# A state-space mixer and a mixture of experts: convolution taps read from PSUM, and the order of one mixer step changed on every engine

## The reference

```
h = layernorm(x) * (1 + ca) + sa
x = x + ga * mixer(h)            # state-space mixer
h = layernorm(x) * (1 + cb) + sb
x = x + gb * moe(h)              # 64 experts, top 8 of 4 of 8 groups, and a shared one

mixer(h): xn = rmsnorm(h); z, xBC, dt = xn @ in_proj.T      # 1024 | 1280 | 16 columns
  xBC = silu(sum_k pad(xBC)[k : k+L] * conv_w[:, k] + conv_b)   # 4 taps along the sequence
  xs, B, C = xBC (1024 | 128 | 128);  dt = softplus(dt + dt_bias)
  y = ssd(xs * dt, dt * A, B, C) over chunks of 128 tokens; y += D * xs
  y = rmsnorm(y * silu(z));  return h + y @ out_proj.T
moe(h): scores = sigmoid(h @ w_router); pick 8 experts; sum of weighted silu(gate) * up @ down
```

## Time and profile before

| what | value |
|---|---|
| median of three runs | 6409.36 us |
| the profiled execution | 6412.97 us |
| its span, first to last instruction | 6411.1 us |
| TensorE busy | 5781.9 us (90%) |
| VectorE busy | 3957.1 us (62%) |
| POOL busy | 3763.9 us (59%) |
| ScalarE busy | 2733.7 us (43%) |
| mean granted TensorE clock | 0.951 |

### The profile page before, as it was taken

How to read it: one execution, slowest core, us unless ns; L and a number is a source line. 1 busy time by engine, 2 the same in 40 slices (tenths; PEclk the granted TensorE clock), 3 DMA queues, 4 the chain that set the end, 5 groups by cost and what they waited for, 6 DMA issues and landing times. The chain is left out here.

```text
span 6411.1 us, 109995 instructions
## 1 busy us (share of the span) xinstructions
PE 5781.9 (90%) x28797; PEld 4345.1 (68%) x28798; DVE 3957.1 (62%) x10033; ACT 2733.7 (43%) x5780; POOL 3763.9 (59%) x2980
## 2 busy tenths in 40 slices
PE   2888888888888888888859999999999999999899
PEld 0556555565565565565548888888788888888787
DVE  1888888888888888888834444444344444444355
ACT  1555555555555555555513333333333333333322
POOL 0466666666666666666645555555555555555477
PEclk8899999999999999999979999999999999999999
DMA  9243343333343333333348887887877777887687
GB/s 351 107 124 119 106 131 120 111 130 107 117 136 105 119 125 105 122 122 105 129 123 194 196 217 173 213 196 175 228 155 176 186 164 179 211 214 196 106 269 256
DMA packets 338146, 1028.39 MB, mean 160 GB/s; under 512 B 55060, under 2 KB 59412, under 8 KB 337124
## 3 DMA queue, kind: packets, MB, share of 16 engines
q1 hardware_dynamic: 175512, 669.44, 30.3%
q0 software_dynamic: 145568, 321.56, 25.7%
q10 hardware_dynamic: 16816, 34.37, 1.4%
HBM read 580.45 MB, written 444.74 MB: 160 GB/s over the span
## 5 line engine op out<-in xcount | busy, mean ns | idle before, releaser
L1324 POOL DMA_INDIRECT acc_dram<-y_e,ids x576 | 907.9, 1576 | 1115.6 <-ACT y_e L1397 680.3
L1205 PE MATMUL bank<-w_hi,x_hi 128*128 (+1 forms) x2560 | 1058.0, 413 | 0.0
L1205 PE MATMUL bank<-w_hi,x_lo 128*128 (+1 forms) x2560 | 1002.3, 392 | 0.0
L1205 PE MATMUL bank<-w_lo,x_hi 128*128 (+1 forms) x2560 | 1001.5, 391 | 0.0
L938 DVE SCALAR_TENSOR_TENSOR acc<-raw,conv_w,acc 128x128 f32<-128x128 f32 x1920 | 820.3, 498 | 7.3 <-ACT acc L665 7.3
L602 POOL DMA_INDIRECT list_dram<-tok_id,pos x512 | 633.3, 1237 | 155.9 <-issue 154.6
L1415 DVE TENSOR_TENSOR h_lo<-bank,h_hi 128x256 fp32r<-128x256 f32 x576 | 243.5, 423 | 753.5 <-ACT h_hi L1386 746.8
L1397 ACT ACTIVATE y_e<-bank,xg_e 128x512 f32<-128x512 f32 x576 | 396.4, 688 | 693.4 <-PE bank L1205 649.1
L1316 POOL DMA_INDIRECT xg_e<-h_dram,ids x576 | 572.0, 993 | 195.0 <-issue 174.1
L1391 ACT ACTIVATE th_f<-bank 128x256 f32<-128x256 f32 x576 | 221.3, 384 | 1017.6 <-PE bank L1205 964.1
L770 PE MATMUL bank<-xn_t,w_in 128*128 128x128 f32 x5120 | 590.5, 277 | 66.4 <-ACT xn_t L644 66.4
(11 more groups left out here) (248 smaller groups left out, 10997.2 us busy)
## 6 DMA issues: line engine op xcount, KB each, us to landing
hi_dram<-w_hi_m SPq DMA_DIRECT2D x130, 768.0 KB, 7.4
lo_dram<-w_raw SPq DMA_DIRECT2D x130, 768.0 KB, 8.8
w_hi<-hi_dram SPq DMA_DIRECT2D x130, 768.0 KB
w_lo<-lo_dram SPq DMA_DIRECT2D x130, 768.0 KB
w_raw<-in_w_experts_dram SPq DMA_DIRECT2D x128, 768.0 KB
acc_dram<-zeros ACTq DMA_DIRECT2D x2, 16640.0 KB, 102.5
acc_c<-acc_dram SPq DMA_DIRECT2D x128, 256.0 KB, 3.5
h_dram<-h SPq DMA_DIRECT2D x64, 288.0 KB
```

Source lines behind the costliest of these rows:

```text
L1205: last = nc.tensor.matmul(acc, a, b, start=(i == 0), stop=(i == len(terms) - 1))
L1324: pool.indirect_dma_start(acc_dram[r % NACC], bass.IndirectOffsetOnAxis(ap=ids[:, r:r + 1], axis=0), y[:, r % YSLOTS, :], None, compute_op ...
```

## The change

- `raw` in SBUF goes. `xn_t` gets three more columns ahead of its 128, in which the last three of the chunk before are kept (`carry`, scaled by `starts`), and each projection tile is computed for 131 columns. The ten tiles lie in PSUM in four groups of 3, 3, 3 and 1 (`half(1)`, `half(0)`, `half(6)`, `half(7)`), dt beside the last; all taps read them there.
- ScalarE's copies to `raw` go, and its first tap is in four parts. `gm` is made in place in PSUM. `gz` has two buffers.
- VectorE: the carry comes first; the first half of the weight split comes behind the early statistics; routing comes ahead of the y chain, whose `state` is made behind `yadd`.
- TensorE: the xr transposes come ahead of `rows`, the projections behind; the h2 transposes ahead of the last group; then router, `ydiag`, `yoff` (which waits for all taps and dt), states, z in the other order of waits, y transposes, rank (now in `half(6)`), and the eight x transposes of the next chunk, ahead of the output projection.
- ScalarE: the copy of `xn_t` comes right behind `xt`, the exponentials of `lm` ahead of `hn2`, the tanh of z and the copy of `y_t` ahead of the square of y. POOL: the list entries come ahead of `r2`.

```diff
-        raw = sb("raw", [P, 2, NE, TAPS - 1 + P])
+        xn_t = sb("xn_t", [P, KD, TAPS - 1 + P])
...
+        XGROUPS = 4
+        OLD = TAPS - 1
...
+        def group(g):
+            return range(3 * g, min(3 * g + 3, NE))
+
+        def raw_of(i):
+            return half((1, 0, 6, 7)[i // 3])[:, i % 3 * (OLD + P):(i % 3 + 1) * (OLD + P)]
...
@@ ScalarE @@
+                        nc.scalar.copy(xn_t[:, :, OLD:], half(0).rearrange("p (k t) -> p k t", k=KD)).then_inc(S["xnT_sb"], 1)
...
-                        act.wait_ge(S["xbc_ps"], 3 * f + g + 1)
-                        n = (4, 4, 2)[g]
-                        nc.scalar.copy(raw[:, 1 - p, 4 * g:4 * g + n, TAPS - 1:],
-                                       half(1 - g % 2)[:, 0:n * P].rearrange("p (n t) -> p n t", n=n)).then_inc(S["raw_sb"], 1)
...
-                        act.wait_ge(S["raw_sb"], 3 * f + g + 1)
+                        act.wait_ge(S["xbc_ps"], XGROUPS * f + g + 1)
                         at_least(act, S["xbc_done"], f)
-                        for i in range(4 * g, min(4 * g + 4, NE)):
-                            last = nc.scalar.activation(acc[:, i, :], raw[:, 1 - p, i, 0:P], ACT.Identity,
+                        for i in group(g):
+                            last = nc.scalar.activation(acc[:, i, :], raw_of(i)[:, 0:P], ACT.Identity,
                                                         bias=conv_b[:, i:i + 1], scale=conv_w[:, i, 0:1])
...
@@ TensorE @@
+                        at_least(pe, S["rank_done"], c - 1)
...
+                        for g in range(XGROUPS):
+                            if g == 2 and c is not None:
+                                pe.wait_ge(S["l_exp"], 2 * c + 1)
+                            if g == 3 and t is not None:
+                                transposes()
+                            for i in group(g):
+                                m = DI + i * P
+                                for k in range(KD):
+                                    last = nc.tensor.matmul(raw_of(i), w_in[:, k, m:m + P],
+                                                            xn_t[:, k, :], start=(k == 0), stop=(k == KD - 1))
...
+                        if f is None:
+                            pe.wait_ge(S["l_exp"], 2 * c + 1)
+                        else:
+                            pe.wait_ge(S["taps"], XGROUPS * (f + 1))
+                            pe.wait_ge(S["dt_raw"], f + 1)
                         at_least(pe, S["state_done"], c)
                         for j in range(2):
                             last = nc.tensor.matmul(bank[3][:, j * 512:(j + 1) * 512], xbc[:, p, 9, :],
...
-                            pe.wait_ge(S["raw_sb"], 3 * f + 2 + j)
-                            if j == 1:
-                                pe.wait_ge(S["dt_raw"], f + 1)
+                            pe.wait_ge(S["taps"], XGROUPS * f + 2 - j)
...
+                    if f is not None:
+                        pe.wait_ge(S["xbc_done"], f + 1)
+                        at_least(pe, S["rank_done"], f - 2)
+                        at_least(pe, S["yadd_done"], f)
+                        for i in range(KI):
+                            last = nc.tensor.transpose(bank[1][:, i * P:(i + 1) * P], xbc[:, 1 - p, i, :], ident[:])
+                        last.then_inc(S["xtok_ps"], 1)
...
@@ VectorE @@
+                    if f is not None:
+
+                        at_least(dve, S["z_ps"], 2 * f)
+                        ts(xn_t[:, :, 0:OLD], xn_t[:, :, P:P + OLD], col(starts, f), None, ALU.mult).then_inc(S["carry"], 1)
...
-                        tt(gm[:], half(4)[:, 0:P], tri[:], ALU.mult)
+                        tt(half(4)[:, 0:P], half(4)[:, 0:P], tri[:], ALU.mult)
...
-                                        last = stt(out=acc[:, i, :], in0=raw[:, 1 - p, i, k:k + P], scalar=conv_w[:, i, k:k + 1],
+                                    for i in group(2 * g + hf):
+                                        last = stt(out=acc[:, i, :], in0=raw_of(i)[:, k:k + P], scalar=conv_w[:, i, k:k + 1],
                                                    in1=acc[:, i, :], op0=ALU.mult, op1=ALU.add)
```

More of the change, by code:

```diff
@@ L640, in step @@
                         nc.scalar.activation(btok[:], half(4)[:, P:2 * P], ACT.Copy, scale=col(ends, c)).then_inc(S["btok_sb"], 1)
-                    if f is not None:
-                        act.wait_ge(S["xnT_ps"], f + 1)
-                        at_least(act, S["z_ps"], 2 * f)
-                        nc.scalar.copy(xn_t[:].rearrange("p k t -> p (k t)"), half(0)).then_inc(S["xnT_sb"], 1)
+                    if c is not None:
+                        for j in range(2):
+                            act.wait_ge(S["rows_ps"], 2 * c + j + 1)
+                            nc.scalar.activation(lm[:, j * DI:(j + 1) * DI], (bank[3] if j == 0 else bank[1])[:], ACT.Exp).then_inc(S["l_exp"], 1)
                     if t is not None:
@@ L701, in step @@
                     if f is not None:
[L702 removed]
+                        act.wait_ge(S["taps"], XGROUPS * (f + 1))
                         at_least(act, S["yoff_ps"], f - 1)
@@ L730, in step @@
                     if c is not None:
-                        pe.wait_ge(S["xbc_done"], c + 1)
-                        at_least(pe, S["rank_done"], c - 1)
-                        at_least(pe, S["yadd_done"], c)
-                        for i in range(KI):
-                            last = nc.tensor.transpose(bank[1][:, i * P:(i + 1) * P], xbc[:, p, i, :], ident[:])
-                        last.then_inc(S["xtok_ps"], 1)
                         at_least(pe, S["yT_sb"], c)
@@ L783, in step @@
                     if c is not None:
-                        pe.wait_ge(S["l_exp"], 2 * c + 1)
+                        pe.wait_ge(S["btok_sb"], c + 1)
+                        pe.wait_ge(S["small_sb"], c + 1)
+                    if f is not None:
+                        pe.wait_ge(S["xnT_sb"], f + 1)
+                        at_least(pe, S["gz_done"], 2 * f)
+                        for g in range(XGROUPS):
[5 more added lines that the diff above has]
+                                m = DI + i * P
+                                for k in range(KD):
+                                    last = nc.tensor.matmul(raw_of(i), w_in[:, k, m:m + P],
+                                                            xn_t[:, k, :], start=(k == 0), stop=(k == KD - 1))
+                            if g == XGROUPS - 1:
+                                for k in range(KD):
+                                    last = nc.tensor.matmul(half(7)[:, 2 * P:2 * P + NH], xn_t[:, k, OLD:],
+                                                            w_in[:, k, DIN - NH:DIN], start=(k == 0), stop=(k == KD - 1))
+                            last.then_inc(S["xbc_ps"], 1)
@@ new lines, in step @@
+                    if f is None and t is not None:
+                        transposes()
+                    if t is not None:
+                        pe.wait_ge(S["h2T_sb"], t + 1)
+                        if c is not None:
+                            pe.wait_ge(S["m_done"], 2 * c + 2)
+                        for k in range(KD):
+                            last = nc.tensor.matmul(half(4)[:, RT:RT + EXPERTS], h2_t[:, k, :], w_router[:, k, :],
+                                                    start=(k == 0), stop=(k == KD - 1))
+                        last.then_inc(S["rt_ps"], 1)
@@ new lines, in step @@
+                    if c is not None:
+                        pe.wait_ge(S["x1s_done"], c + 1)
+                        pe.wait_ge(S["m_done"], 2 * c + 2)
+                        for hh in range(NH):
+                            last = nc.tensor.matmul(bank[1][:, hh * HD:(hh + 1) * HD], lm[:, hh * P:(hh + 1) * P],
+                                                    x1s[:, hh * HD:(hh + 1) * HD], start=True, stop=True)
+                        last.then_inc(S["ydiag_ps"], 1)
+                    if c is not None:
+                        if f is None:
[3 more added lines that the diff above has]
+                            pe.wait_ge(S["dt_raw"], f + 1)
@@ L790, in step @@
                         last.then_inc(S["yoff_ps"], 1)
-                        pe.wait_ge(S["btok_sb"], c + 1)
-                        pe.wait_ge(S["small_sb"], c + 1)
-                    if t is not None:
-                        pe.wait_ge(S["h2T_sb"], t + 1)
-                        for k in range(KD):
-                            last = nc.tensor.matmul(half(4)[:, RT:RT + EXPERTS], h2_t[:, k, :], w_router[:, k, :],
-                                                    start=(k == 0), stop=(k == KD - 1))
-                        last.then_inc(S["rt_ps"], 1)
                     if c is not None:
@@ L924, in step @@
                         early.end()
+                    if ws is not None:
+                        split_lo(dve, ws, 0)
                     if f is not None:
```

174 lines of the change are left out of this document (68 added, 106 removed).

## The result

The changed kernel takes 6048.08 us (median of 4 runs, 6044.02 to 6051.27) against 6409.47 us for the kernel before, measured beside it: a ratio of 0.9437, interval 0.9421 to 0.9453, so 361 us less. The forecast was 6013 in a range of 5930 to 6180. The profiled execution has a span of 6049.3 us.

A forecast was written before the change was run, and what follows sets the result against it. A step was TensorE's work at full clock (39.2 us), 2.2 of half clock and 5.95 of waits, mostly for late VectorE. The step falls by 6.3 to 41.5; 63 chunks give 396 us: 6013, range 5930 to 6180.

The forecast's parts named there:

- Part 1: VectorE: taps read PSUM and no longer wait for POOL; 4.8 us a step go, PSUM source taken as free.
- The rival in which the taps still wait: VectorE's last twelve taps still wait for POOL, 4 us ahead of `yoff`: step 45.3, 6256 us; chance 6%.
- Part 2: VectorE: `gm` in PSUM frees the two `lm` products of the lock, 1.89 to 1.21 each, 1.3 us a step.
- Parts 3, 4, 9 and 10: ScalarE's `raw` copies go (0.41 us a tile); 131-column streams, earlier POOL list entries, later half weight split: taken as nothing.
- the slower rival: TensorE reads odd-word `xn_t` rows in twice the time, 9.0 us: step 50.5, 6580 us; chance 4%.
- Part 5: TensorE: `rows` ahead of the projections covers the `xn_t` copy; the 1.00 us wait goes, 0.3 idle for `x1` comes.
- Part 6: VectorE: routing ahead of the y chain, `picked` 6 us early; TensorE's 2.96 us wait goes, `y` is late next.
- the walk: One mixer step timed from the projections' start: z and `y` end at 26.6, next projections start at 41.2 us.
- part 8: TensorE: `yoff` waits for all 30 taps, covered by router and `ydiag`, 4.5 us; the walk has 0.9 idle.
- Part 7: TensorE: eight x transposes ahead of the output product cover the `yT` copy (1.0 us); 0.2 to 0.5 idle.
- The clock: TensorE in the mixer: no wait over a microsecond, so clock taken as full and its 2.2 us as gained.
- the clock still falls: TensorE's clock falls to half between z and the output product: step 43.9, 6164 us; chance 15%.

The follow-up runs named there:

- taps_sbuf: Changed kernel with VectorE's thirty taps reading a tile in SBUF instead of the projections in PSUM (convolution not computed); 6375.2 us, ratio 0.9947 to the kernel before.
- xtok_back: Changed kernel with the eight x transposes moved from ahead of the output product to the start of the next step; 6049.8 us.
- z_between: Changed kernel with the first half of the z product moved from behind states to between router and `ydiag`; 6028.1 us.
- all_four: Changed kernel with states ahead of `ydiag`, dt's Abs on ScalarE, POOL's `xt * d_skip` behind third list entry, VectorE's first weight-split half in the output-product wait; 5998.4 us.

## Why the prediction was right, and where it was off

The time lies in the stated range, and none of the three signs of being wrong came: no tap over 1 us, no 131-column matmul over 120 ns, no clock of 0.50 in every step. Both theories of the experiments hold in part: undoing the taps costs 327 us, `gm` 277, the xr transposes 157, routing 150, the x transposes nothing. These add up to far more than 361, so none of them is a share of the gain; each part is worth its price only with the others in place.

**Part 1, the taps: right.** 4.8 us a step was forecast; between 1800 and 2342 us VectorE was busy 141.4 us with 330 taps of the kernel before, 11 steps, or 12.9 a step; now it is 102.0 / 12.9 = 7.9, so 4.9 less. The price of a PSUM source, taken as nothing, is nothing: 338 ns a tap, one every 0.26 us, from PSUM in the changed kernel and from SBUF in taps_sbuf. The 65 ns that the section on the TRN2 errata of "VectorE: DVE Perf Modes" in the Trainium skill would have added (an estimate) are not there. The rival in which the taps still wait is out.

**Part 2, `gm` in PSUM: right on VectorE, mis-sized by a factor.** 1.3 us a step was put down, and VectorE's two products do take 2.4 instead of 3.7. But with `gm` back in SBUF the step is 4.4 us longer. The part's worth lies on POOL, whose short operations stand at the head of the chain to `h_t` (1.6 us), and in the clock (most of the rest). The prediction priced the lock by its VectorE side alone.

**VectorE's total: 36.6 us for a forecast 35 to 36.** The two parts are worth 4.9 + 1.4 = 6.3, and 4.6 came. Most of the rest was given back to collisions with POOL: the first half of the weight split, whose mean with the other half rose from 1812 to 2127 ns (0.6 us a step), `sp_a` from 1.05 to 1.58, `acs` from 0.83 to 1.02. That the split could collide was named; the others weren't.

**Parts 3, 4, 9 and 10: right.** ScalarE is busy 23.1 us a step and stays covered, POOL's `r2` is through before the output product ends, and no weight split waits for its load. The products with 131 columns take 8.27 / 72 = 115 ns, those with 128 took 9.20 / 80 = 115, and nothing shows that odd rows cost anything; the slower rival is out.

**Part 5: right.** Its 1.00 is gone, its new wait is 0.41 for a forecast 0.3. Undone, it costs 157 us, two and a half times the 63 that a wait of 1.0 is worth: a step without a fall is 2.0 us longer (1.07 for the copy, 0.48 more for `x1`, 0.18 more at the router make 1.7 of it), and twelve more falls of the clock come with it.

**Part 6: right.** The 2.96 is gone, and `y` is what is late next. In the step shown, with its projections starting 41.47 ahead of 1991.36, `y` ended at 26.9 for the walk's 26.6. That this is so close is luck: the taps ended 0.8 early, and the stall of `sp_a`, which the walk did not have, took it back. z ended at 25.7, not 26.6, since **part 8** was wrong: the taps ended at 14.9 instead of 15.7, and `yoff` did not wait for them. The time stood at the y transposes instead, as 1.33 us.

**Part 7: worth nothing.** It covers the `yT` copy as said, and the loop over VectorE doesn't care. What it did for the clock between z and the output product (no fall there, 12 without it) came back as falls elsewhere: 19 in the narrow run against 8.

**The clock: the step that failed.** "No wait is over a microsecond, so I take the clock as full": the 2.2 us of half clock behind z are gained as forecast, and the two transposes with rank between z and the output product do not make a trough. The rule of the Trainium skill in "TensorE: Matmul & The Clock Gate", Part 4, that transposes don't count as matmuls do, did not decide here: in the changed kernel no fall lies in that stretch, though it has a wait of 1.33 us too, and with the x transposes taken out of it (xtok_back) 12 falls do. Transposes there were better than idleness, whatever they count. A few falls do come: z_between has the same waits in this stretch and four of them. The clock falls in 19 steps elsewhere, in the narrow run. That is 30 us of the 35 by which 6013 was short. The rival "the clock still falls" had 15%, at another place and in every step, for 151 us; what came is a fifth of that.

## What to carry to other kernels

Price an operation that shares the lock from both sides: what it waits, and what the other engine's chain waits behind it, down to operations of one column; moving one operand to PSUM can be worth more on the engine that you did not touch. Look for the loop over engines that closes a step (here 32 us of VectorE and 9.4 of TensorE): moves that leave it alone (the x transposes) bring nothing, and moves into its idle part (half a weight split) do. When TensorE is at last full, look at which of its products are narrow and stand in a row: here half a z product between them was worth 20 us and no work.

## What was not expected of the hardware

- The clock of TensorE fell to half 2.6 us after TensorE's last gap (0.22 us), in a run of products of 16 and 64 columns: in 19 of 62 steps; not once in that run with half a z product in it, 13 times and for half as long with the states product, and never in `all_four`. Why it is 19 and not 62 stays open. The falls come at a beat: 13 of the 18 distances between them are 126.3 us, three steps, the others two or four steps. So how often a kernel meets them may hang on the length of its step too; that was not tested, though z_between has the same undisturbed step as the changed kernel.
- A stream of thirty VectorE operations with both inputs in SBUF kept a POOL multiplication of 1.27 us out for 6.71.
- POOL operations of one column wait too (2.14 us for 0.27), and so did a VectorE operation with a single SBUF input (1.72 us for 0.18).
- A product of 131 columns out of rows of odd length costs what one of 128 does, 115 ns.
